# Layer-0 channel attention of a two-layer decoder: the projection is folded into a mixing matrix per batch, in place of two further products

## The reference

```
h = (x - mu) / sqrt(var + 1e-5) * norm_w + norm_b
q, k, v = split(h @ qkv_w.T + qkv_b)            # each 256 tokens x 256 channels
w = softmax(einsum('ncq,nck->nqk', q, k / 16), axis=2)
a = einsum('nqk,nck->ncq', w, v)                # tokens x channels
return a @ proj_w.T + proj_b + x
```

## Time and profile before

| | |
|---|---|
| median of 3 runs | 3640.21 us (3635.18 to 3641.67) |
| profiled execution, its own time | 3634.66 us |
| span of its instructions | 3633.0 us |
| PE busy over the span | 79% |
| DVE, ACT, POOL busy | 62%, 42%, 18% |
| mean granted TensorE clock | 0.896 |
| first stage, layer-0 attention | from 45.6 to 439 us |

### The profile page before, as it was taken

The page is one execution under the profiler, slowest core; times in us unless marked ns, Lnnn a source line. Parts: engine busy times, 40 slices in busy tenths (PEclk is TensorE's granted clock), DMA queues, the critical chain, the costliest instruction groups (busy, mean ns, idle before and its releaser), DMA issues. The chain is left out here.

```text
span 3633.0 us, 60719 instructions
## 1 busy us (share of the span) xinstructions
PE 2876.1 (79%) x21702; PEld 2244.0 (62%) x21703; DVE 2268.1 (62%) x3977; ACT 1511.0 (42%) x2470; POOL 667.5 (18%) x640
## 2 busy tenths in 40 slices
PE   4999877777655699999206999879999999177796
PEld 3666555555445588888205888756666666166686
DVE  5554557777644211111456888879999999778542
ACT  1233244434311122222004666568888888178000
POOL 0111103333346201001570000021111110000600
PEclk9999988888855799999658999889999999699898
DMA  3000051111132444444230000000000000034444
GB/s 110 0 0 0 20 205 53 53 53 53 36 123 96 151 145 141 145 142 141 86 102 27 1 1 1 1 31 13 13 13 13 13 13 7 25 162 185 173 150 162
DMA packets 109948, 259.90 MB, mean 72 GB/s; under 512 B 15040, under 2 KB 52928, under 8 KB 101056
## 3 DMA queue, kind: packets, MB, share of 16 engines
q1 hardware_dynamic: 91712, 204.85, 16.4%
q0 software_dynamic: 18048, 52.45, 4.4%
HBM read 169.17 MB, written 88.08 MB: 71 GB/s over the span
## 5 line engine op out<-in xcount | busy, mean ns | idle before, releaser
L1765 DVE TENSOR_SCALAR e_low<-bank 128x2048 f32<-128x2048 f32 x128 | 293.1, 2290 | 37.1 <-PE bank L1637 34.0
L1159 ACT ACTIVATE cx_h<-bank,c_b 128x256 f32<-128x256 f32 x288 | 120.7, 470 | 409.6 <-PE bank L1114 409.6
L1114 PE MATMUL bank<-cx_zT,cx_w 128*128 128x256 f32 x1152 | 262.5, 381 | 1.8 <-DMA cx_w<-cw_dram 0.9
L1125 PE MATMUL bank<-c_w,cx_h 128*128 x1152 | 260.4, 379 | 0.0
L1589 ACT ACTIVATE e_low<-e_low 128x2048 f32<-128x2048 f32 x128 | 245.1, 1915 | 2.1
L1586 ACT ACTIVATE e_low<-e_low 128x2048 f32<-128x2048 f32 x128 | 243.5, 1903 | 0.0
L1114 PEld LDWEIGHTS bank<-cx_zT,cx_w 128*128 128x128 f32 x1152 | 220.3, 191 | 32.3 <-DMA cx_w<-cw_dram 1.3
L2131 PE MATMUL bank<-f_wout,fd_q 128*128 128x256 f32 x1024 | 224.2, 383 | 19.6 <-DVE fd_q L2150 19.6
L1125 PEld LDWEIGHTS bank<-c_w,cx_h 128*128 128x128 f32 x1152 | 213.6, 190 | 25.9
L2131 PEld LDWEIGHTS bank<-f_wout,fd_q 128*128 128x128 f32 x1024 | 196.7, 192 | 46.9 <-DVE fd_q L2150 19.8
L1766 DVE TENSOR_SCALAR e_high<-bank 128x1536 f32<-128x1536 f32 x128 | 223.8, 1749 | 0.0
(11 more groups left out here) (362 smaller groups left out, 6781.9 us busy)
## 6 DMA issues: line engine op xcount, KB each, us to landing
cx_w<-cw_dram SPq DMA_DIRECT2D x72, 512.0 KB, 3.2
hidden<-fu_h SPq DMA_DIRECT2D x32, 1024.0 KB, 3.9
fd_h<-hidden SPq DMA_DIRECT2D x32, 1024.0 KB, 4.8
cx_rows<-expert_rows SPq DMA_DIRECT2D x72, 256.0 KB, 3.2
slot_y<-cx_y POOLq DMA_DIRECT2D x72, 256.0 KB, 2.5
X<-x_dram SPq DMA_DIRECT2D x4, 2048.0 KB, 16.0
g_cT<-ctxT_dram SPq DMA_DIRECT2D x32, 256.0 KB, 5.4
queries<-g_qT SPq DMA_DIRECT2D x32, 256.0 KB, 6.2
```

What stands on the lines that cost most here:

```text
L1114: last = nc.tensor.matmul(H[k][f // 2][:, (f % 2) * GROUP_ROWS:(f % 2 + 1) * GROUP_ROWS], w1[k][:, c, f * P:(f + 1) * P], zT[k][:, c, :], ...
L1125: last = nc.tensor.matmul(Y[k][:, n * D:(n + 1) * D], h[k][:, f, n * P:(n + 1) * P], w2[:, bass.ds(e, 1), f, :].rearrange("p o d -> p (o d ...
L1159: nc.scalar.activation(h[k][:, f, :], H[k][f // 2][:, (f % 2) * GROUP_ROWS:(f % 2 + 1) * GROUP_ROWS], ACT.Gelu, bias=b1[:, bass.ds(e, 1), ...
L1765: nc.vector.tensor_scalar(flat(low[n % RING][:]), HEADS4.rearrange("p r s -> p (r s)"), -1.0, 0.0, ALU.mult, ALU.max).then_inc(neg_ready, 1)
```

## The change

Mixing and projection are both linear, so their order is free. Let E be the exponentials before they are divided by their row sums, and R the reciprocals of the sums. The kernel before computes (v' E^T R) W. The changed one computes v' (E^T (R W)). Here v' is tokens by channels and W is the projection.

- ACT scales the projection's rows by the reciprocals, for each batch, into `shares` (`L210` of the changed kernel), from SBUF, right behind the exponentials. The eviction `L211` goes.
- PE multiplies the exponentials, as they lie, with `shares` into `qB(p)[0]` (four matmuls of 256 columns a batch, `L257`). The four transposes a batch (`L258`) go, and so does the product with v at that place (`L266`).
- DVE copies this result, `mixer`, out of PSUM (`L326`), where it copied the transposed exponentials. Both reciprocals now stand ahead of both copies.
- `project` multiplies `vT` with `mixer` (four matmuls of 256 columns a batch, `L267`), where it multiplied `aT` with the projection. It waits for `mixer_ready` and `v_ready`.

```diff
@@ scalar, middle(i)
                 for p in range(PAIR):
-                    act.wait_ge(a_raw, batch_of(i, p))
                     act.wait_ge(rsum_ready, batch_of(i, p))
                     for c in range(DC):
-                        nc.scalar.activation(aT[p][:, c, :], qB(p)[1][:, c * S:(c + 1) * S], ACT.Identity,
-                                             scale=rsum[:, p, c:c + 1]).then_inc(a_ready, 1)
+                        nc.scalar.activation(shares[p][:, c, :], wproj[:, c, :], ACT.Identity,
+                                             scale=rsum[:, p, c:c + 1]).then_inc(shares_ready, 1)
@@ tensor, middle(i)
                 for p in range(PAIR):
-                    pe.wait_ge(e_ready, batch_of(i, p) * DC)
+                    pe.wait_ge(shares_ready, batch_of(i, p) * DC)
                     for k in range(DC):
                         for q in range(DC):
-                            last = nc.tensor.transpose(qB(p)[0][:, k * D + q * P:k * D + (q + 1) * P],
-                                                       e[p][:, q, k * P:(k + 1) * P], t["ident"][:])
-                    last.then_inc(eT_raw, 1)
-                for p in range(PAIR):
-                    pe.wait_ge(eT_ready, batch_of(i, p))
-                    pe.wait_ge(v_ready, batch_of(i, p) * DC)
-                    for q in range(DC):
-                        for k in range(DC):
-                            last = nc.tensor.matmul(qB(p)[1][:, q * S:(q + 1) * S], eT[p][:, k, q * P:(q + 1) * P], vT[p][:, k, :],
-                                                    start=k == 0, stop=k == DC - 1)
-                    last.then_inc(a_raw, 1)
+                            last = nc.tensor.matmul(qB(p)[0][:, k * D:(k + 1) * D], e[p][:, q, k * P:(k + 1) * P], shares[p][:, q, :],
+                                                    start=q == 0, stop=q == DC - 1)
+                    last.then_inc(mixer_raw, 1)
 
             def project(i):
                 for p in range(PAIR):
-                    pe.wait_ge(a_ready, batch_of(i, p) * DC)
+                    pe.wait_ge(mixer_ready, batch_of(i, p))
+                    pe.wait_ge(v_ready, batch_of(i, p) * DC)
                     for n in range(TB):
-                        for q in range(DC):
-                            last = nc.tensor.matmul(vB(p)[:, n * D:(n + 1) * D], aT[p][:, q, n * P:(n + 1) * P], wproj[:, q, :],
-                                                    start=q == 0, stop=q == DC - 1)
+                        for k in range(DC):
+                            last = nc.tensor.matmul(vB(p)[:, n * D:(n + 1) * D], vT[p][:, k, n * P:(n + 1) * P], mixer[p][:, k, :],
+                                                    start=k == 0, stop=k == DC - 1)
                     last.then_inc(o_raw, 1)
@@ vector, middle(i)
                 for p in range(PAIR):
                     dve.wait_ge(e_ready, batch_of(i, p) * DC)
                     nc.vector.reciprocal(rsum[:, p, :], esum[:, p, :]).then_inc(rsum_ready, 1)
-                    dve.wait_ge(eT_raw, batch_of(i, p))
-                    nc.vector.tensor_copy(eT[p][:], qB(p)[0][:].rearrange("p (c k) -> p c k", c=DC)).then_inc(eT_ready, 1)
+                for p in range(PAIR):
+                    dve.wait_ge(mixer_raw, batch_of(i, p))
+                    nc.vector.tensor_copy(mixer[p][:], qB(p)[0][:].rearrange("p (c k) -> p c k", c=DC)).then_inc(mixer_ready, 1)
```

More of the change, by code:

```diff
@@ L152, in layer0_attention @@
         esum, rsum = sb("esum", [P, PAIR, DC]), sb("rsum", [P, PAIR, DC])
-        eT = [sb(f"eT{p}", [P, DC, D]) for p in range(PAIR)]
-        aT = [sb(f"aT{p}", [P, DC, S]) for p in range(PAIR)]
+        shares = [sb(f"shares{p}", [P, DC, D]) for p in range(PAIR)]
+        mixer = [sb(f"mixer{p}", [P, DC, D]) for p in range(PAIR)]
         res = [sb(f"res{p}", [P, TB, D]) for p in range(PAIR)]
@@ L159, in layer0_attention @@
         sc_raw, ntop_ready, e_ready = sem("sc_raw"), sem("ntop"), sem("e")
-        eT_raw, eT_ready, rsum_ready = sem("eT_raw"), sem("eT"), sem("rsum")
-        a_raw, a_ready, o_raw, x_done = sem("a_raw"), sem("a"), sem("o_raw"), sem("x_done")
+        mixer_raw, mixer_ready, rsum_ready = sem("mixer_raw"), sem("mixer"), sem("rsum")
+        shares_ready, o_raw, x_done = sem("shares"), sem("o_raw"), sem("x_done")
         res_scaled, res_ready, v_steps = sem("res_scaled"), sem("res"), sem("v_steps")
```

## The result

The changed kernel takes 3690.24 us (median of 4 runs, 3685.81 to 3692.96), the kernel before 3639.92 us beside it (3635.18 to 3641.67). The ratio is 1.0139, with a 95% interval of 1.0122 to 1.0157: 50 us slower. That is inside the range of the prediction (3672 to 3722), 10 us under its value of 3700.

A forecast was written before the change was run, and what follows sets the result against it. The prediction took PE to bound the first stage, with one idle place a trip. The profiled 3634.7 us + 35 of waits + 25 of clock gave 3695 us, or 3700 us on the median, range 3672 to 3722.

The forecast's parts named there:

- What bounds the stage: First stage: PE is the bound, busy 368.6 of 395 us, with one idle place in each trip.
- First wait: PE ahead of the mixer: scaling on ACT behind the second batch's exponentials starts it 0.41 us later, in 16 trips.
- Both waits: PE ahead of the mixer and ahead of `z`'s transposes: 2.31 us in each of 15 trips, 35 us in all.
- The clock, 25 us: PE slows to half clock after 3.0 us idle ahead of the mixer: 1.6 us a trip, 25 us.
- the second wait: PE ahead of `turn`: `z` is late because DVE's second copy waits for the whole second mixer; 1.9 us a trip.
- The reading behind it: Second stage: six transposes take 0.85 us behind 2.01 us idle, 1.51 us behind 2.75 or 2.76, so the clock falls.
- The signs: First-stage timeline: trips of 26.6 us at full clock, 28.2 with its share; mean clock about 0.9; most mixers over 3.6 us.
- The clock holds: Rival for the first stage: both waits come and nothing else, 3640 + 35 = 3675 us; 17%.
- Not slower: Rival between exponentials and product: the path shortens by the removed transposes, 0.50 us in 16 trips, 3632 us; 4%.
- the first wait alone: Rival: `z` is ready in time, so only 16 x 0.41 = 7 us ahead of the mixer stay, 3647 us; 4%.
- Sum: Whole kernel: 3634.7 us profiled, + 35 of waits, + 25 of clock, 3695 us; 3700 us on the median.

The follow-up runs named there:

- E7: Changed kernel with sixteen unused transposes a trip filling PE's idle place ahead of the mixer; ratio 1.0092 to the kernel before, on a second chip.
- E1: Changed kernel with the four DVE instructions that write `z` put ahead of both mixer copies; 3655.87 us, ratio 1.0048 to the kernel before.
- E2: Changed kernel with the first batch's scaling on ACT ahead of the second batch's exponentials; 3685.2 us, ratio 1.0127 to the kernel before.
- E6: Changed kernel with `z` ahead of the mixer copies on DVE and eight unused transposes a trip in PE's idle place; 3650.23 us, ratio 1.0033.
- E8: Changed kernel with sixteen unused transposes a trip in PE's idle place and `z` ahead of the mixer copies; ratio 1.0017, on a second chip.
- E9: Kernel before, old algebra, with `z` ahead of the row maxima, its transposes in PE's idle place and the v product in `zB`; 3625.75 us, ratio 0.9966.
- E5: Changed kernel with next pair's `z` transposes in PE's idle place, `z` before row maxima, first batch's scaling before second's exponentials; ratio 0.9969, second chip.
- E3: Changed kernel with eight unused transposes of the exponentials a trip put back into PE's idle place; 3680.52 us, ratio 1.0113 to the kernel before.
- E4: Changed kernel with the next pair's `z` transposes in PE's idle place and `z` written ahead of the row maxima; ratio 0.9998, on a second chip.

## Why the prediction was right

The path was right step by step, and so was the sign; one term was too large.

- *What bounds the stage: right.* PE's own chain through the trip, with one idle place.
- *First wait, 0.41 us: measured 0.40.* From the start of the scaling to the first matmul of the mixer I had 0.94 us, and it is 0.95 (258.85 to 259.80); the 0.1 us for the weights is there too. My sum has a slip of 0.02: 236.73 and 0.1 are 236.83, not 236.85.
- *Both waits, 2.31 us a trip: measured 2.26,* and E7 gives 34 us for the 16 trips where the sum had 35. The chain named is the one in the trace: second copy behind the mixer, `z` behind the copy, transposes behind `z`. E1 takes it away by DVE's order alone.
- *The clock, 25 us: measured 14.* That is the mis-sized term; that the clock would fall there was right. The 1.6 us a trip was two thirds of 2.5, an average over 16 trips. Measured it is 0.9: nine slow mixers of 1.4 to 1.7 us. Both parts were too large. A slow mixer stands for about 3 us at half clock, where I had taken 4.9 us from the second stage, and only nine trips of 16 have one. Nothing of it falls into the second wait, as I had thought part would. The step that failed is carrying the second stage's price over to this one. There PE is busy with short operations between its idle times; here 18 us of work without a gap, from the transposes of `z` to the scores, lie ahead of the mixer's idle place.
- *The reading behind it.* I compared 2.01 us, fast, with 2.75 and 2.76, slow, as if the clock changed between them. Six other rows with 2.00 us are slow (E2 above), so the length of the one idle time did not make this contrast. That the new idle time was long enough came out right all the same.
- *The signs.* The mean clock is 0.97 over the window of the earlier trace rows, where I named about 0.9. That did not fit my own term either: 25 us lost are 50 us at half clock, about 0.94 over the stage. And "over 3.6 us" could not tell a slow mixer, since the fast ones take 3.72.
- *The clock holds, 3675 us (17%):* the size of this case, 35 us, is met by E7 with 34, once the idle time is filled. By the rule of thumb of the Trainium skill (TensorE: Matmul & The Clock Gate, "HAM oscillation — how this bites in real kernels") an idle time of 2.8 us would leave the clock alone. The trace does not agree: nine mixers behind 2.83 us are slow, and in E2 fourteen behind 2.0 us.
- *Not slower, and the first wait alone:* E6 and E8 are the second of these with the order put right, 11 and 7 us by their medians and ratios, where I had 7.
- *Sum:* 35 + 25 against 34 + 14 in the stage, and 3700 against 3690 us. The 10 us between them are nearly all in the clock's term.

What I would read otherwise now: idle time on the bounding engine is a place to put work, and the change had just freed the bank for it (E9 found the room in the kernel before as well). I had worked out that PE would be idle for 3.0 us there, and that the wait for `z` ahead of `turn` would cost 1.9 us some 4 us later, and did not put the two together.

## What to carry to other kernels

Count an instruction as removed from the path only if the engine was not going to wait there anyway; here 128 transposes went and 50 us came. When a copy is made to wait for a longer product, look at what stands behind it on its engine, and who waits for that: independent work such as the next pair's normalisation belongs ahead of such a wait. And before algebra is changed to save work on the bounding engine, try the order: the same idle place, filled with the next trip's transposes, gave the old kernel 13 us.

## What the hardware showed that I had not expected

- The clock of TensorE fell with no single idle time over 1.07 us (E6, three of sixteen trips), and did not fall with 1.15 us in one piece and little around it (E5), nor with 0.3 and 0.2 us (E8). So one piece alone does not decide it. Counted from start to start, as for E3, all idle time between scores and mixer is 1.3 us or less in E5, E7 and E8 and 1.8 us in the kernel before, without a fall in the loop; it is 2.1 us or more in every variant with one. The six slow rows behind 2.00 us in the second stage, each with another idle time shortly ahead, fit this: idle time near the place seems to count together.
- Above that more idle time does not mean more falls. By the bracket ahead of the mixer, and slow mixers: 2.83 us, nine of 16 (changed) and seven of 16 (E1); 2.02 us, fourteen of 16 (E2); 1.96 us, two of 15 (E4). What sets which trips are slow stays open.
- Because of this, a change that shortens a wait by 0.8 us (E2), and the trip at full clock by 0.5, won little: the stage ends 2.3 us earlier, and the medians are 5 us apart with intervals of the ratios that overlap, where 8 were to be had at full clock.
- On the second chip the kernel before is 52 us slower. In E7's trace the third stage's routing part takes 234 us there, against 202 us in the profiled execution of the kernel before, which is 32 of the 52. The trips of the first stage are as long as on the first chip. Why is not shown.
